# Rounding a feed-forward block's high part on ScalarE by applying the Gelu twice

## The reference

```python
x = x + 0.5 * ffn(layernorm(x), w1, b1, w2, b2)
x = x + attn(layernorm(x), ...)
x = x + 0.5 * ffn(layernorm(x), w1, b1, w2, b2)

def ffn(x, w1, b1, w2, b2):              # 256 -> 1024 -> 256
    h = gelu(x @ w1 + b1, approximate=False)
    return h @ w2 + b2
```

## Time and profile before

| | |
|---|---|
| median of three executions | 1430.82 us |
| profiled execution: time | 1438.96 us |
| its span, first to last instruction | 1437.3 us |
| busy: PE, PEld | 1162.0, 836.3 us |
| busy: DVE, ACT, POOL | 837.3, 503.4, 390.5 us |
| granted clock of TensorE over the span, share of full speed | 0.886 |
| Gelu of the feed-forward blocks (L558) | 128, 88.1 us busy, 689 ns each |
| cast to the high part (L1255) | 128, 69.5 us busy, 543 ns each |
| subtract to the low part (L1256) | 128, 129.8 us busy, 1014 ns each |
| up steps (L730 to L732, 512 columns, up and projections) | 120.0, 112.5, 112.0 us busy |
| down steps (L730 to L732, 256 columns with `h`) | 154.7, 147.4, 147.7 us busy |

### The profile page before, as it was taken

How to read it: one execution, slowest core, us unless ns; L and a number is a source line. 1 busy time by engine, 2 the same in 40 slices (tenths; PEclk the granted TensorE clock), 3 DMA queues, 4 the chain that set the end, 5 groups by cost and what they waited for, 6 DMA issues and landing times.

```text
span 1437.3 us, 27174 instructions
## 1 busy us (share of the span) xinstructions
PE 1162.0 (81%) x10172; PEld 836.3 (58%) x10172; DVE 837.3 (58%) x1534; ACT 503.4 (35%) x809; POOL 390.5 (27%) x597
## 2 busy tenths in 40 slices
PE   4766688889878988789887998689887898788847
PEld 3633574378535875378634785268743785367626
DVE  5752266665666556565666657664666657644354
ACT  2142135323343335323353324423353234531222
POOL 6008200750018300560008400380007500281000
PEclk9888798889989999889988999889999899877678
DMA  4040103110040201210030200401030100401000
GB/s 131 16 88 1 29 16 69 21 29 17 15 89 1 45 16 46 43 29 18 15 89 0 45 1 16 89 16 31 16 71 18 29 16 1 88 1 43 1 0 16
DMA packets 80265, 47.47 MB, mean 33 GB/s; under 512 B 55808, under 2 KB 73728, under 8 KB 80128
## 3 DMA queue, kind: packets, MB, share of 16 engines
q1 hardware_dynamic: 80128, 45.56, 13.9%
HBM read 30.86 MB, written 14.68 MB: 32 GB/s over the span
## 4 chain that ended last, share of the span: by engine, by line
PE 50%; DVE 29%; issue 8%; ACT 6%; SPq 3%; POOL 2%; DMA 1%; DVEq 1%; ACTq 0%; POOLq 0%
PE psum L730 10%; PE psum L731 9%; PE psum L732 9%; DVE conv_acc L1276 7%; PE psum L761 3%; DVE h_lo L1256 3%; DVE arena L1501 3%; PE psum L1021 2%; PE psum L911 2%; PE psum L900 2%; DVE arena L1233 2%; SPq L336 2%; PE psum L1090 1%; DVE bn L1221 1%; DVE arena L1503 1%
## 5 line engine op out<-in xcount | busy, mean ns | idle before, releaser
L505 POOL TENSOR_TENSOR l_prod<-arena 64x30 f32<-64x30 f32 (+14 forms) x240 | 142.9, 595 | 776.3 <-DMA arena<-l_dram 758.1
L558 ACT ACTIVATE h_f<-psum,b_col 128x512 f32<-128x512 f32 x128 | 88.1, 689 | 291.7 <-PE psum L732 227.8
L730 PE MATMUL psum<-w_hi,h_hi 128*128 128x256 f32 x512 | 154.7, 302 | 32.3 <-DVE h_lo L1256 32.3
L1021 PE MATMUL psum<-v_shift,fir_w 128*32 128x512 f32 x1152 | 144.1, 659 | 10.7 <-DMA v_shift<-v_dram 10.6
L509 POOL TENSOR_TENSOR arena<-arena,l_prod 64x30 f32<-64x30 f32 (+14 forms) x240 | 145.3, 605 | 18.8
L732 PE MATMUL psum<-w_hi,h_lo 128*128 128x256 f32 x512 | 147.7, 288 | 0.0
L731 PE MATMUL psum<-w_lo,h_hi 128*128 128x256 f32 x512 | 147.4, 288 | 0.0
L730 PE MATMUL psum<-xt_hi,w_hi 128*128 128x512 f32 x256 | 120.0, 469 | 32.2 <-DVE xt_lo L1242 14.0
L1256 DVE TENSOR_TENSOR h_lo<-h_f,h_hi 128x512 fp32r<-128x512 f32 x128 | 129.8, 1014 | 4.4
L1255 DVE CAST h_hi<-h_f 128x512 fp32r<-128x512 f32 x128 | 69.5, 543 | 103.5 <-ACT h_f L558 51.4
L1276 DVE SCALAR_TENSOR_TENSOR conv_acc<-psum,conv_col,conv_acc 128x511 f32<-128x511 f32 x144 | 107.8, 748 | 36.8 <-ACT conv_acc L583 18.4
(11 more groups left out here) (221 smaller groups left out, 2255.1 us busy)
## 6 DMA issues: line engine op xcount, KB each, us to landing
x_in<-in_L_attn_x SPq DMA_DIRECT2D x8, 512.0 KB, 3.4
v_dram<-v_fm SPq DMA_DIRECT2D x8, 512.0 KB, 2.8
v_shift<-v_dram SPq DMA_DIRECT2D x8, 512.0 KB, 5.0
out<-x_tok SPq DMA_DIRECT2D x8, 512.0 KB, 4.4
v_shift<-v_dram SPq DMA_DIRECT2D x8, 511.0 KB, 7.1
v_shift<-v_dram SPq DMA_DIRECT2D x8, 510.0 KB, 9.0
v_shift<-v_dram SPq DMA_DIRECT2D x8, 509.0 KB, 11.7
arena<-in_L_ffn_w SPq DMA_DIRECT2D x2, 1024.0 KB, 7.1
```

What stands on the lines that cost most here:

```text
L505: pool.tensor_tensor(prod, l_inv[:, k + 1:, k:k + 1].broadcast_to(shape), l_inv[:, k:k + 1, 0:k].broadcast_to(shape), ALU.mult).then_inc(i ...
L558: act.activation(h_f[:, m % 2, :], bank, ACT.Gelu, bias=b1_col[:, m:m + 1]).then_inc(read, 1)
L730: pe.matmul(dst, a_hi, b_hi, start=first, stop=False, **kw)
L1021: last = pe.matmul(banks[p][0][col:col + 32, :], fir_w[:, group, n, :], v_shift[:, group, at_t:at_t + T], start=(n in (0, TAPG)), stop=(n ...
```

## The change

ACT applies the Gelu twice from the same PSUM bank: once to `h_f` in fp32, once to `h_hi`, whose type rounds it. DVE's cast goes, and its subtract reads both. The wait for `h_used`, which protects the buffer of `h_hi` and `h_lo`, moves from DVE to ACT, ahead of the second Gelu. The bank is set free by the second Gelu. `DVE_STEPS` counts fewer links.

```diff
@@ -308,7 +308,7 @@
-        DVE_STEPS = {"head": 47, "body": 80, "last": 75, "tail": 38}
+        DVE_STEPS = {"head": 39, "body": 64, "last": 59, "tail": 30}
@@ -555,7 +555,10 @@
                 if m >= 2:
                     act.wait_ge(h_split[f], KT * seq + m - 1)
 
-                act.activation(h_f[:, m % 2, :], bank, ACT.Gelu, bias=b1_col[:, m:m + 1]).then_inc(read, 1)
+                act.activation(h_f[:, m % 2, :], bank, ACT.Gelu, bias=b1_col[:, m:m + 1])
+                if m >= RING:
+                    act.wait_ge(h_used[f], (KT - 1) * seq + m - RING + 1)
+                act.activation(h_hi[:, m % RING, :], bank, ACT.Gelu, bias=b1_col[:, m:m + 1]).then_inc(read, 1)
@@ -1250,9 +1253,6 @@
                 def split(f, seq, m):
                     copied(dve, at, ("upa", "upc")[f], m)
-                    if m >= RING:
-                        dve.wait_ge(h_used[f], (KT - 1) * seq + m - RING + 1)
-                    link(dve.tensor_copy(h_hi[:, m % RING, :], h_f[:, m % 2, :]))
                     dve.tensor_tensor(h_lo[:, m % RING, :], h_f[:, m % 2, :], h_hi[:, m % RING, :].bitcast(F32),
                                       ALU.subtract).then_inc(h_split[f], 1)
```

## The result

Before and after, measured side by side: 1432.3 us (1430.59 to 1435.53, four executions) and **1475.9 us** (1468.36 to 1479.66, four). The ratio is **1.0295, 95% interval 1.0249 to 1.0341**: slower, as predicted, but by some 44 us instead of 24, and 8 us above the range's upper end of 1468. The profiled execution of the changed kernel took 1475.62 (span 1473.9, clock 0.874).

What follows compares the result with a forecast made beforehand. The prediction took the kernel as bound by the order of PE's work, with waits for DVE. Terms +30.0, +0.3, -1.8, -4.1, +4.7 and -4.7 gave +24.4, from 1430.82 to 1455.2 us, range 1440 to 1468.

Steps and rivals of the forecast that it cites:

- gap ahead of the first tile: At each later pass's start, PE waits for ACT's x_t copy before the first tile: 1.43 us, in seven passes.
- gaps in the tiles less the gain at down 6: In those passes' tiles, PE waits of 1.02, 1.13, 0.14 and 1.02 us, less 0.45 from an earlier subtract.
- clock, block A: Feed-forward block at a later pass's start: PE's clock falls in all seven passes, three more than before: +4.7 us.
- block C: end, POOL and clock: Feed-forward block at a pass's end: +0.3 us at the last down steps, -4.1 from POOL, -4.7 from fewer clock falls.
- head: First feed-forward block, beside the preparation of weights: four casts fewer on DVE, -1.8 us.
- the 0.09 that the prediction took off: Weight load already shown before the recurrence steps, subtracted from the gaps at L890 and L907: 0.09 us each.
- the 0.14 at the bank: At a later pass's start, after down 4, up 7 waits 0.14 us for Gelu 6 to release bank 2.
- a rival with a chance of 0.15: Clock also falls behind the first new gap, 1.43 us, at each later pass's start: seven falls, +10.9, 1466 us; chance 0.15.
- the subtract will be held in the same place: At a pass's end, DVE's subtract still stands still beside POOL's large steps, up to 7 us, so PE's stall stays.
- the 0.6 that POOL was to gain: At a pass's end, three casts fewer during POOL's inversion shorten PE's stall by 0.6 us, in all -4.1.
- the second rival: At a pass's end, the stall goes altogether because POOL comes past in time: 11.4 us less, 1444 us; chance 0.12.
- The base: Whole kernel: +24.4 us put the profiled 1438.96 at 1463.4; the unprofiled median 1430.82 gave 1455.2.

Runs made afterwards that it cites:

- ring3: The changed kernel with three buffers of h_hi and h_lo instead of two: 1415.17 us, ratio 0.9854.
- reorder: The changed kernel, two buffers, with ACT doing the next recurrence copy ahead of the second Gelu and its wait at each later pass's start: 1414.57 us, ratio 0.988.
- fill_first: The changed kernel with 7 useless matmuls on PE ahead of the first tile's gap only, the other gaps left unfilled: 1456.64 us, ratio 1.0129.
- a_only: The kernel before with the change only in the head and at the start of later passes; the block at a pass's end keeps DVE's cast: 1484.38 us, ratio 1.0351.

## Why the prediction was wrong in size

The direction, the place and the mechanism of the gaps were right: ACT's queue holds PE in block A, and both ways of lifting that (ring3, reorder) turn the loss into a gain. The size failed by a term, the clock in block A. In the steps of the prediction, for the profiled execution in us:

| term | predicted | measured |
|---|---|---|
| gap ahead of the first tile, seven times | +10.0 | +11.5 |
| gaps in the tiles less the gain at down 6 | +20.0 | +22.5 |
| clock, block A | +4.7 | +17.3 |
| block C: end, POOL and clock | -8.5 | -15.2 |
| head | -1.8 | +0.3 |
| middle of the passes, and the tail | 0 | +0.2 |
| sum | +24.4 | +36.6 |

- **The gaps** were right one by one: 1.43, 1.02, 1.13, 1.02 and 1.12 predicted, 1.66 (1.56 and 1.82 occur), 1.03, 1.14, 1.03 and 1.10 measured. In the first, PE starts 0.46 (0.36 to 0.62) behind the end of ACT's copy, where the sum had 0.14; why it takes longer there than at L893 stays open. At full clock a tile stretch is 32.47 (fill_first's third pass, the gaps in its tiles unfilled) for 29.25, that is +3.22 where 3.31 - 0.45 = 2.86 were forecast: from start to start, set against ring3, the three gaps cost 1.11, 1.21 and 1.11, some 0.08 more than the idle time, which is the 0.09 that the prediction took off; the 0.14 at the bank came as forecast.
- **The step that failed is the clock in block A.** I took three falls more than before, all at the end of the block, and gave the fall behind the first gap to a rival with a chance of 0.15, because no row below 1.57 showed one. The gap was 1.66, and the clock fell behind it in six of seven passes, and again at the block's end in seven of seven: thirteen falls for four. In a_only, the same block A, it fell behind the first gap in four of seven. Three of the thirteen also lasted about twice as long as the others, both of the first pass and the last one of the second. In the rows below (columns as above) the first two are the long falls of the first pass, the other two short ones in the third and the last pass, each in 7 us:

```profile
174.70:181.70 7.00, 7.00 (x37) 6.00 (x38) 1.17 (x3) 1.11 (x3) 0.00 (x0) 0.62 0.00 0
203.00:210.00 7.00, 5.90 (x32) 5.76 (x30) 4.31 (x10) 1.53 (x3) 0.00 (x0) 0.54 0.00 0
520.30:527.30 7.00, 6.93 (x42) 5.64 (x42) 1.13 (x3) 1.08 (x3) 0.00 (x0) 0.76 0.01 2
1227.00:1234.00 7.00, 6.16 (x40) 6.02 (x39) 3.18 (x7) 1.53 (x3) 0.00 (x0) 0.76 0.00 0
```

Nine more falls, with three of the thirteen long, make the 17.3, which is 11 times 1.56 and not 3 times. The two places were not alternatives: the rival's 10.9 came on top of the forecast's 4.7, which makes 15.6. The rows that were looked at were also too few. The trace of the kernel before has a fall behind gaps of 0.96 and 1.03 that stand close together (and some 4 us behind one of 1.73), in a stretch outside blocks A and C:

```profile
1079.14 0.63 PE L761 MATMUL psum<-ident,stat_fm 128*128 128x128 f32 x4 [0.96 <-ACT stat_fm L562]
1080.80 4.48 PE L1021 MATMUL psum<-v_shift,fir_w 128*32 128x512 f32 x24 [1.03 <-DMA v_shift<-v_dram]
```

```profile
1080.80:1084.50 3.70, 3.70 (x20) 1.05 (x24) 3.28 (x8) 0.15 (x1) 0.00 (x0) 0.54 0.45 71
```

- **Block C** gave 6.7 more. The step that failed is "the subtract will be held in the same place", and with it the 0.6 that POOL was to gain. POOL gained nothing: from the first product of its inversion to L519 it took 42.1 us on average, for 42.0 before. What changed is the instruction that it catches. The cast of step 3, at 11.3 us behind the block's first product, is gone, and the subtract behind it stands at 11.7 to 12.1, where POOL's first large step, at 9.6 to 13.7, comes sometimes before and sometimes after it; in the pass shown 0.09 us of order decide over a stall of 1.9. The time was partly that of the second rival (0.12), the mechanism was not: that rival wanted POOL to come past by being quicker. So two effects that were held unlikely came together, with opposite signs, and hid a part of each other; without the one in block C the total would have been further off. A subtract was held here too (5.07 for 0.69), as the trace of before has it. The rule cited there, of the Trainium skill, "GPSIMD Engine Reference", section Specifications, agrees with that; which instruction is held it can't tell.
- **The head's** 1.8 did not show (156.9 us for 156.6), and a head that differs by 5.6 between two traces of the same code can't show it.
- **The base.** The prediction moved the sum from the profiled execution (1438.96) to a median 8 us lower (1430.82). The changed kernel's profiled run took 1475.62 with a median of 1475.89. The kernel before ranges over 1423.8 to 1442.9 in eighteen executions of one comparison, so which of its times is the base is itself open by some 8 us. That alone puts 8 of the 20.7 missing in the median; the terms above are the other 12.
- **What stays open:** why the falls of passes one and two last longer (tile stretches of 38.12 and 36.86 for 35.4), why a gap of 1.66 has a fall in one pass and none in another, and why the last gaps' falls mostly vanish when the first gap is filled.

## What to carry to other kernels

An instruction that is moved to another engine takes its wait along, and everything written behind it on that engine waits too. Ask which of these the critical engine needs next, and put them ahead of the wait or give the buffer one more copy: the same change lost 3% in one order and gained 1.2% in another. A gap in front of TensorE is worth more than its length, since the clock can fall behind it, so gaps near the length at which one row shows a fall should be priced with the fall, each of them, and not only the last, and gaps that stand close together count too. And where two engines share something, look at which instruction comes first within a few tenths of a microsecond, as any saving ahead of it can turn the order, for better or worse.

## What the runs showed of the hardware

- Useless matmuls in the gaps made the kernel 24 us faster (1475.9 to 1451.6), by keeping the granted clock at 1.00 over block A for 0.90; one pass of the tiles takes 32.4 instead of 35.4 us.
- 64 more matmuls a pass on TensorE brought a wait of about 6 us in each of six passes that no semaphore explains, 36.0 us in all, and one packet of an instruction queue lands in each of them, 1.3 to 1.5 us ahead of its end; 15 more matmuls brought no such wait. That the packet is the cause is not shown.
- A gap of TensorE of 1.66 was followed by a fall of the granted clock in some passes and by none in others (all five in the changed kernel, one of three in a_only), and two gaps of 1.03 and 1.10 that stand some 1 us apart by one in all seven passes (in two of seven with the first gap filled); a fall cost about 1.56 us, in three of thirteen cases about twice that.
- An instruction on VectorE that meets POOL's large steps waits: a cast of 0.43 took 2.42 over the first of them, the subtract behind it 4.57 over the rest, another subtract 5.07 for 0.69; where POOL pauses between them, it is held through one alone (the cast took 2.03 beside a copy of 2.09).
